# Macaron block on one core: the dense projection in fp16 parts set into the end of attention, and the QKV bias as rows of TensorE's accumulation

## What is computed

```
x = x + 0.5 * ffn(layernorm(x))
x = x + attn(layernorm(x))
x = x + 0.5 * ffn(layernorm(x))

ffn:  W = base + mean|w - base| * sign(w - base)          (for w1, w2, w3; inner width 1792)
      silu(h @ W1.T) * (h @ W3.T) @ W2.T
attn: qkv = h @ w_qkv.T + b_qkv                           (768 columns: 32 query heads, 8 key and 8 value heads of 16)
      q, k = rope(q), rope(k);  p = softmax(causal(q @ k.T / 16));  ctx = p @ v
      out = ctx @ w_dense.T + b_dense                     (512 x 512)
```

## Time and profile before

| | |
|---|---|
| median of 3 runs | 1591.55 us (1591.51 to 1592.71) |
| profiled execution, its own time | 1593.44 us |
| span of the profiled execution | 1591.7 us |
| PE / DVE / ACT / POOL busy | 1468.1 / 886.1 / 629.0 / 151.2 us |
| QKV stage (first QKV matmul to last evicted tile) | 531.48 to 618.42 |
| first score piece | 626.90 |
| VectorE ends groups 0, 1, 2 and 15 | 654.81, 682.22, 707.80, 1040.40 |
| iterations 16 and 17 begin; first projection matmul | 1041.27; 1075.04 |
| second feed-forward block begins | 1143.78 |

### The profile page before, as it was taken

The page is one execution under the profiler, slowest core; times in us unless marked ns, Lnnn a source line. Parts: engine busy times, 40 slices in busy tenths (PEclk is TensorE's granted clock), DMA queues, the critical chain, the costliest instruction groups (busy, mean ns, idle before and its releaser), DMA issues.

```text
span 1591.7 us, 24945 instructions
## 1 busy us (share of the span) xinstructions
PE 1468.1 (92%) x9552; PEld 660.3 (41%) x9552; DVE 886.1 (56%) x1387; ACT 629.0 (40%) x887; POOL 151.2 (10%) x217
## 2 busy tenths in 40 slices
PE   0778999899999895799999999989999999999998
PEld 0233444344445453334343434324444444444443
DVE  7979432432444587899999999923431422412212
ACT  4464111121222133388888888771211212112111
POOL 0320000000000243012121212210000000000000
PEclk9989999899999987599999999999999999999999
DMA  9501800000000000000000000024000000000000
GB/s 388 195 0 53 353 0 0 1 0 0 1 1 0 1 1 34 1 3 2 2 2 3 2 2 2 2 94 185 0 0 0 27 0 0 27 0 0 27 0 27
DMA packets 16459, 57.38 MB, mean 36 GB/s; under 512 B 4848, under 2 KB 4848, under 8 KB 15856
## 3 DMA queue, kind: packets, MB, share of 16 engines
q1 hardware_dynamic: 16368, 56.11, 9.1%
HBM read 40.63 MB, written 15.20 MB: 35 GB/s over the span
## 4 chain that ended last, share of the span: by engine, by line
PE 80%; DVE 12%; ACT 4%; issue 3%; DMA 1%; POOL 0%; DVEq 0%; SPq 0%; ACTq 0%; POOLq 0%
PE ps L1222 32%; PE ps L1243 16%; PE ps L1478 9%; PE ps L1393 7%; PE ps L1459 5%; PE ps L1576 3%; PE ps L1269 2%; PE ps L1216 1%; DVE w_all L870 1%; DVE rowmax L1110 1%; PE ps L1488 1%; PE ps L1355 1%; DVE w_raw L829 1%; DVE wbase L864 1%; ACT parts_q L665 1%
## 5 line engine op out<-in xcount | busy, mean ns | idle before, releaser
L1222 PE MATMUL ps<-xt_hi,w_all 128*128 128x512 f16 x896 | 284.3, 390 | 41.4 <-DVE w_all L870 19.3
L693 ACT ACTIVATE probs<-ps 128x1024 f32<-128x1024 f32 (+3 forms) x384 | 294.2, 814 | 48.7 <-PE ps L1459 45.7
L1110 DVE TENSOR_REDUCE rowmax<-ps 128x2 f32<-128x1024 f32 (+3 forms) x208 | 237.0, 1140 | 16.0 <-PE ps L1401 7.5
L958 DVE SCALAR_TENSOR_TENSOR hb<-ps,scal,silub 128x512 f32<-128x512 f32 x56 | 42.0, 750 | 266.6 <-PE ps L1222 266.6
L1393 PE MATMUL ps<-ka,qa 48*128 48x512 f16 (+3 forms) x768 | 165.6, 345 | 15.4 <-DVE rowmax L1110 9.2
L1222 PE MATMUL ps<-xt_lo,w_all 128*128 128x512 f16 x448 | 174.6, 390 | 0.0
L1478 PE MATMUL ps<-probs,vs 128*32 128x512 f32 (+3 forms) x1536 | 164.5, 500 | 1.6 <-ACT ctx_sb L712 1.1
L1222 PEld LDWEIGHTS ps<-xt_hi,w_all 128*128 128x128 f16 (+1 forms) x896 | 89.7, 100 | 155.5 <-issue 41.3
L1114 DVE TENSOR_REDUCE rowmax<-ps 128x1 f32<-128x512 f32 x192 | 131.1, 683 | 16.3 <-PE ps L1393 13.5
L1459 PE MATMUL ps<-qa,ka 50*128 50x512 f16 (+3 forms) x768 | 133.2, 330 | 3.7 <-ACT probs L693 2.8
L1243 PE MATMUL ps<-w32b_all,hhib 128*128 (+1 forms) x448 | 133.3, 379 | 0.0
(11 more groups left out here) (148 smaller groups left out, 2151.7 us busy)
## 6 DMA issues: line engine op xcount, KB each, us to landing
spill<-w_all SPq DMA_DIRECT2D x1, 10752.0 KB, 28.8
w32b_all<-spill SPq DMA_DIRECT2D x1, 7168.0 KB, 19.6
x<-x_in SPq DMA_DIRECT2D x4, 1024.0 KB, 5.4
y_out<-x SPq DMA_DIRECT2D x4, 1024.0 KB, 4.2
wbase<-m1t SPq DMA_DIRECT2D x4, 896.0 KB, 12.6
w_raw<-w1t SPq DMA_DIRECT2D x4, 896.0 KB, 14.1
wbase<-m3t SPq DMA_DIRECT2D x4, 896.0 KB, 24.3
w_raw<-w3t SPq DMA_DIRECT2D x4, 896.0 KB, 24.3
```

The lines of the kernel that those rows point to most:

```text
L693: nc.scalar.activation(probs[u % PBUF][:, 2 * pair:2 * pair + 2, 0:q1 - q0], wide(("scores", g, (u, pair)))[:, :, 0:q1 - q0], ACT.Exp, sca ...
L958: nc.vector.scalar_tensor_tensor(out=bufs["h"][u][:, :], in0=ps[:, UP, :], scalar=scal[:, 1:2], in1=bufs["silu"][u][:, :], op0=ALU.mult, o ...
L1110: nc.vector.tensor_reduce(dst, src, AX.X, ALU.max).then_inc(pair_taken, 1)
L1222: last = mm(ps[:, bank, :], w[a][:, k, bass.ts(t, P)], xt[b][:, k, :], start=(k == 0 and n == 0), stop=(k == HB - 1 and n == 2))
```

## The change

The change has two parts.

**The QKV bias.** VectorE's `add_bias` goes. Two fp16 rows' worth of bias (`brow`, 64 partitions: the high part and the remainder) are made by three VectorE instructions late in chunk 2, and `qkv(i)` begins each half with one more matmul of `row_ones` by `brow`. ScalarE's new `take_raw(i)` evicts the tile with the scale, ahead of `v_all(i)` in its order. In chunk 1 the maximum over the bias moves ahead of `power_of_two(3)`, and one small operation is added. `along(i)` waits for the low parts of tile i-2 too.

**The dense projection.** `wd` is held as two fp16 parts and the context too, in three passes: 12 matmuls of 512 columns for a tile. The maximum over `wd` is a VectorE instruction after iteration 0 (`dense_bound`), the scale a chain of nine after iteration 1 (`dense_scale`); GpSimd waits for the maximum ahead of its loop. GpSimd makes the high parts in iteration 2 (`dense_high`, two instructions for each of four blocks, between `copy_v(2)` and `mask_unit(1, 2)`) and the low parts in iteration 3 (`dense_low`, one for each of four, at the same place); SyncE moves them into place with four transfers after group 4's. The column of ones that gives the softmax sums is scaled by GpSimd. TensorE's and VectorE's iterations 16 and 17 are written out with tiles 0 to 7 of the projection between the pieces of attention, with one PSUM bank for the transposes and one for the results; VectorE makes both parts of these tiles' contexts. Tiles 8 to 15 follow attention, with ScalarE making the high part and VectorE the low one.

The diff, without semaphore declarations and with the written-out order cut:

```diff
-    mrow = at("mrow", [8 * SEQ_TILES, P], F16, C0 + 6144)
...
-    wd = at("wd", [P, HB, HID], F32, R0)
+    wd_raw = at("wd_raw", [P, HB, HID], F32, R0)
+    wd_at = [at(f"wd_at{i}", [P, 2, HID], F16, a) for i, a in enumerate((D0 + 6144, D0 + 14336, B0 + 30720, C0 + 6144))]
+    wd = [at(f"wd_{n}", [P, HB, HID], F16, R0 + 4096 * i) for i, n in enumerate(("hi", "lo"))]
...
-    ctx_t = [at(f"ctx_t{i}", [P, HB, P], F32, R0 + 10240 + i * 2048) for i in range(2)]
+    ctx_t = [[at(f"ctx_t{n}{i}", [P, HB, P], F16, R0 + 10240 + i * 2048 + j * 1024) for j, n in enumerate(("hi", "lo"))]
+             for i in range(2)]
...
+    def rows_bank(i):
+
+        return PAIR_BANK if i < SEQ_TILES else PAIR_BANK + i % 2
+
+    def dense_bank(i):
+
+        return PAIR_BANK + 1 if i < SEQ_TILES else i % 2
...
+            if g == 4:
+                sp.wait_ge(wdlo_ready, HB)
+                for i in range(2):
+                    for n in range(2):
+                        sp.dma_start(wd[i][:, 2 * n:2 * n + 2, :], wd_at[2 * i + n][:, :, :]).then_inc(wd_placed, 16)
 
...
+                chain(nc.gpsimd.memset(vs[i][:, :, HEAD:HEAD + 1], 1.0))
+                nc.gpsimd.tensor_scalar(vs[i][:, :, HEAD:HEAD + 1], vs[i][:, :, HEAD:HEAD + 1], wc[:, 4, 4:5], None,
+                                        ALU.mult).then_inc(ones_ready, 1)
...
+        def dense_high(n):
+
+            if n == 0:
+                pool.wait_ge(wd_scaled, 1)
+            chain(nc.gpsimd.tensor_scalar(wd_raw[:, n, :], wd_raw[:, n, :], wc[:, 3, 3:4], None, ALU.mult))
+            nc.gpsimd.tensor_copy(wd_at[n // 2][:, n % 2, :], wd_raw[:, n, :]).then_inc(wdhi_ready, 1)
+
+        def dense_low(n):
+
+            pool.wait_ge(wdhi_ready, n + 1)
+            nc.gpsimd.tensor_tensor(out=wd_at[2 + n // 2][:, n % 2, :], in0=wd_raw[:, n, :], in1=wd_at[n // 2][:, n % 2, :],
+                                    op=ALU.subtract).then_inc(wdlo_ready, 1)
+
+        pool.wait_ge(part_ready, 5)
+        nc.gpsimd.partition_all_reduce(allr[:, 3, 1:2], part[:, 3, 1:2], P, RMAX).then_inc(allr_ready, 1)
         for k in range(GROUPS + 2):
             mask_unit(k - 2, 7)
             mask_unit(k - 2, 8)
             mask_unit(k - 1, 0)
             mask_unit(k - 1, 1)
             copy_v(k)
+            if k == 2:
+                for n in range(HB):
+                    dense_high(n)
+            if k == 3:
+                for n in range(HB):
+                    dense_low(n)
...
+        def take_raw(i):
+            act.wait_ge(qkv_full, i + 1)
+            if i >= 2:
+                act.wait_ge(v_ready, i - 1)
+                act.wait_ge(rot_ready, i - 1)
+                act.wait_ge(turned_ready, 2 * (i - 1))
+            b0 = 2 * (i % 2)
+            nc.scalar.activation(qkv_raw[i % 2][:, :].rearrange("p (s n) -> p s n", s=2), ps[:, b0:b0 + 2, 0:QKV // 2],
+                                 ACT.Copy, scale=scal[:, 3:4]).then_inc(raw_ready, 1)
...
-        def take_ctx_t(i):
+        def context_high(i):
             act.wait_ge(dt_full, i + 1)
-            if i >= 2:
-                act.wait_ge(dense_full, i - 1)
-            nc.scalar.copy(ctx_t[i % 2][:, :, :].rearrange("p a b -> p (a b)"), ps[:, 4 + i % 2, :])\
-                .then_inc(ctx_t_ready, 1)
-
-        for i in range(TOKEN_TILES):
-            take_ctx_t(i)
+            act.wait_ge(dense_full, i - 1)
+            nc.scalar.copy(ctx_t[i % 2][0][:, :, :].rearrange("p a b -> p (a b)"), ps[:, rows_bank(i), :])\
+                .then_inc(ctx_hi_ready, 1)
+
+        for i in range(SEQ_TILES, TOKEN_TILES):
+            context_high(i)
...
+                    dve.wait_ge(tables_loaded, 48)
+                    chain(nc.vector.tensor_reduce(bqmax[:, :], bq[:, :], AX.X, ALU.max, apply_absolute_value=True))
+                    chain(nc.vector.tensor_scalar(wc[:, 3, 1:2], bqmax[:, :], 1.0 / 64, allr[:, 3, 1:2], ALU.mult, ALU.max))
                     power_of_two(3)
...
                     assert steps[0] == WQ_READY, steps[0]
-                    dve.wait_ge(tables_loaded, 48)
-                    chain(nc.vector.tensor_reduce(bqmax[:, :], bq[:, :], AX.X, ALU.max, apply_absolute_value=True))
+                    chain(nc.vector.tensor_scalar(scal[:, 5:6], wc[:, 3, 3:4], XS / M_UNIT, None, ALU.mult))
...
+                    nc.vector.memset(row_ones[:, :], M_UNIT / 32).then_inc(brow_ready, 1)
+                    dve.wait_ge(brow_ready, 2)
+                    nc.vector.scalar_tensor_tensor(out=brow[32:64, :], in0=bq[32:64, :], scalar=scal[32:64, 5:6],
+                                                   in1=brow[32:64, :], op0=ALU.mult, op1=ALU.subtract).then_inc(brow_ready, 1)
                 for t in (IT - 2, IT - 1):
...
-        def add_bias(i):
-            dve.wait_ge(qkv_full, i + 1)
-            if i >= 2:
-                dve.wait_ge(v_ready, i - 1)
-                dve.wait_ge(turned_ready, 2 * (i - 1))
-            b0 = 2 * (i % 2)
-            nc.vector.scalar_tensor_tensor(
-                out=qkv_raw[i % 2][:, :].rearrange("p (s n) -> p s n", s=2), in0=ps[:, b0:b0 + 2, 0:QKV // 2],
-                scalar=scal[:, 3:4], in1=bq[:, :].rearrange("p (s n) -> p s n", s=2), op0=ALU.mult,
-                op1=ALU.add).then_inc(raw_ready, 1)
-
         def along(i):
             dve.wait_ge(raw_ready, i + 1)
+            if i >= 2:
+                dve.wait_ge(qklo_ready, 2 * (i - 1))
             factor = cos[:, i % SEQ_TILES, :].unsqueeze(1).to_broadcast([P, ROT // HEAD, HEAD])
...
                 along(i)
...
-        for k in range(GROUPS + 2):
+        def dense_bound():
+
+            dve.wait_ge(wd_loaded, 32)
+            nc.vector.tensor_reduce(part[:, 3, 1:2], wd_raw[:, :, :].rearrange("p t n -> p (t n)"), AX.X, ALU.max,
+                                    apply_absolute_value=True)\
+                .then_inc(part_ready, 1)
+
+        def dense_scale():
+
+            dve.wait_ge(allr_ready, 9)
+            chain(nc.vector.tensor_copy(wc[:, 3, 1:2], allr[:, 3, 1:2]))
+            power_of_two(3)
+            chain(nc.vector.tensor_tensor(out=scal[:, 4:5], in0=wc[:, 3, 4:5], in1=wc[:, 4, 4:5], op=ALU.mult))
+            nc.vector.tensor_copy(wc[:, 3, 1:2], allr[:, 3, 1:2]).then_inc(wd_scaled, 1)
+
+        for k in range(GROUPS):
...
-
-
-        dve.wait_ge(wd_loaded, 32)
+            if k == 0:
+                dense_bound()
+            if k == 1:
+                dense_scale()
+
...
+        def context_high(i):
+            dve.wait_ge(dt_full, i + 1)
+            if i >= 2:
+                dve.wait_ge(dense_full, i - 1)
+            nc.vector.tensor_copy(ctx_t[i % 2][0][:, :, :].rearrange("p a b -> p (a b)"), ps[:, rows_bank(i), :])\
...
+        def context_low(i):
+            dve.wait_ge(ctx_hi_ready, i + 1)
+            hi, lo = (t[:, :, :].rearrange("p a b -> p (a b)") for t in ctx_t[i % 2])
+            nc.vector.tensor_tensor(out=lo, in0=ps[:, rows_bank(i), :], in1=hi, op=ALU.subtract).then_inc(ctx_lo_ready, 1)
+
+        def add_dense(i):
             dve.wait_ge(dense_full, i + 1)
             dve.wait_ge(bias_ready, i + 1)
-            nc.vector.tensor_tensor(out=x[:, i, :], in0=ps[:, i % 2, :], in1=x[:, i, :], op=ALU.add).then_inc(x2_ready, 1)
+            nc.vector.scalar_tensor_tensor(out=x[:, i, :], in0=ps[:, dense_bank(i), :], scalar=scal[:, 4:5], in1=x[:, i, :],
+                                           op0=ALU.mult, op1=ALU.add).then_inc(x2_ready, 1)
+
+        context_high(0)
...
+        bias_x(0)
+        bias_x(1)
+        context_high(1)
+        context_low(1)
+        bias_x(2)
+        bias_x(3)
+        add_dense(0)
+        context_high(2)
+        context_low(2)
+        bias_x(4)
+        bias_x(5)
...
+        normalise(15, 1)
+        add_dense(7)
+        context_low(SEQ_TILES)
+        for i in range(SEQ_TILES, TOKEN_TILES):
+            if i + 1 < TOKEN_TILES:
+                context_low(i + 1)
+            add_dense(i)
             if i == 8:
                 layer_norm(8)
             if i in (12, 13):
...
             if i == 1:
...
+                   start=True, stop=False)
                 for k in range(HB):
                     for n, (a, b) in enumerate(PASSES):
                         last = mm(ps[:, 2 * (i % 2) + s, 0:QKV // 2], xt[a][:, k, j * P:(j + 1) * P],
-                                  wq[b][:, k, s * QKV // 2:(s + 1) * QKV // 2],
-                                  start=(k == 0 and n == 0), stop=(k == HB - 1 and n == 2))
+                                  wq[b][:, k, s * QKV // 2:(s + 1) * QKV // 2], start=False,
+                                  stop=(k == HB - 1 and n == 2))
...
-        for k in range(GROUPS + 2):
+        for k in range(GROUPS):
...
             b, tt = divmod(i, SEQ_TILES)
-            if i >= 2:
-                pe.wait_ge(ctx_t_ready, i - 1)
+            if tt % 4 == 0:
+                pe.wait_ge(single_taken, taken(("ctx", GROUPS * (b + 1) // BATCH - 1, tt // 4)))
+            if i == 0:
```

(71 more changed lines are left out.)

131 lines of the change are left out of this document (119 added, 12 removed).

## The result

The changed kernel takes 1614.59 us (median; 1610.61 to 1619.24) against 1591.97 for the kernel before beside it: a ratio of 1.0142, 95% interval 1.0128 to 1.0156. The forecast was 1587.5, a little faster. Two executions of all that are reported here took far longer (2167.0 us of the kernel before, 2510.19 of experiment 5), and the ratios leave them out. Its lines L511, L518, L519 and L524 are GpSimd's mask, `dense_high`'s scaling and cast, and `dense_low`; L1505 is the bias matmul, L1509 the other QKV matmuls, L1607 `values`, L1588 `scores_t`, L1721 `project`, L719 ScalarE's `take_raw`.

A forecast was written before the change was run, and what follows sets the result against it. It took VectorE to bound the QKV stage, a TensorE-VectorE ring attention, and TensorE the feed-forward blocks. Gains of 8.3 and 9.4 us less preparation and stops summed to -4.0 us from 1591.55: 1587.5 us, range 1577 to 1598.

The forecast's parts named there:

- the nearer row: GpSimd, iteration 2: each `dense_high` instruction priced as the mask, 0.634 us, not at `copy_v`'s 1.16, the dearest bound.
- the stop of 2.8: Attention, iteration 2: `dense_high` delays the mask, so TensorE stops 2.8 us ahead of `values(1, 2)`; 2.8 to 6.9 with iteration-2 bounds.
- The first rival: GpSimd's instructions cost as `copy_v`'s elements, TensorE slow after both stops: gain eaten, +9.0 us, 1596.5; chance 0.17.
- First feed-forward block +2.2: Bias preparation in chunks 1 and 2: exposed VectorE operations add 2.2 us (1.5 to 4).
- QKV stage -8.3: QKV stage: TensorE becomes the bound, 26 matmuls of 0.163 us a tile, 4.23; gain 8.3 us (0 to 12).
- `dense_bound` +1.9: VectorE after attention's iteration 0: the maximum over `wd` adds 1.9 us (1 to 2.3).
- `dense_scale` +1.4: VectorE in attention's loop: nine chained operations, 1.7 us, taken as adding 1.4 us (0 to 1.7).
- Start of attention, 0: From the last evicted QKV tile into the first iterations: no change counted, up to 5.5 us to win if the clock holds.
- Iteration 3, +2.9: Attention, iteration 3: `dense_low` on GpSimd, 5.1 us, makes the mask 2.9 us late (2.5 to 4.5).
- Slow returns, one of 2.5: TensorE after the two GpSimd stops and chunk 2's short one: one return at low clock, +2.5 us (0 to 7).
- Tail, 54.3: Iterations 16 and 17 with projected tiles 0 to 7: 54.3 us (52 to 58) instead of 33.8, +20.5.
- Tiles 8 to 15, 38.8: Dense stage behind attention: 38.8 us (35 to 41) instead of 68.7, -29.9; with the tail, -9.4.

The follow-up runs named there:

- experiment 5: The QKV bias part of the change alone, with its 64-row bias matmuls, in the kernel before: 1591.08 us, ratio 0.9990.
- experiment 1: The changed kernel with one tiny GpSimd addition (128x1) right behind the all-reduce of the dense weight's bound: 1608.63 us, ratio 1.0099.
- experiment 3: The changed kernel with the bias in 128 partitions instead of 64, so its matmul has 128 rows: 1610.97 us, ratio 1.0111.
- experiment 2: experiment 1 with GpSimd's dense-weight preparation moved ahead of mask_unit(k-1, 0), into its idle time in iterations 2 to 4: 1596.07 us, ratio 1.0010.
- 7: experiment 2 with the statistics of the second feed-forward block's first LayerNorm taken in the tail: 1584.53 us, ratio 0.9961.
- experiment 6: experiment 2 with the tail's projection quarters issued in pairs, 16 groups of six matmuls instead of 32 of three: 1586.20 us, ratio 0.9968.

## Why the prediction was wrong

The step that failed is GpSimd in iteration 2: "I take the nearer row, the mask: 8 x 0.634 = 5.1 us", and the stop of 2.8 from it. Two things were wrong in it. Four of the eight instructions are scalings, of 1.57 us, dearer than even the far row's 1.16; the four casts, 0.61, are at the near row. Together they take 8.9 us (712.27 to 721.16), and that this lies within the bound of 8 x 1.16 = 9.3 is luck. And 7.37 us for the first arithmetic after an all-reduce stood in no term, nor in the bounds; experiment 1 shows it. Together they made 14.0 us of 2.8. The first rival had the place and the sign; it said that over 0.9 us for an instruction decides, and it was priced without the wait. A page of the Trainium skill that I had not used for this names a cost of this kind: "GPSIMD Engine Reference", section "Instruction dispatch", has the first call of freshly loaded code pay about 6 us that no instruction of the profile shows. Here it was 6.7 to 7.7; that code is loaded in it, no row shows.

The other terms, forecast and measured in the profiled pair:
- First feed-forward block +2.2: right for the stops, 6.54 and 2.29 us for 6.29 and 0.34. The QKV stage starts only 0.6 us later, because 0.9 was gained at the very start, ahead of the change's first instruction, and the lower clock behind the first stop ended sooner and took 0.8 less (granted clock 0.94 for 0.71 between 290 and 295 us).
- QKV stage -8.3: -2.4. ScalarE and the slow return were right, and nearly so the stop ahead of `qkv(6)` (5.1 forecast, 4.28). "26 x 0.163" took a 64-row matmul at its neighbours' rate; it costs 0.2 us more, 6 us in the stage. With 128 rows the term is right to 0.3 us (experiment 3).
- `dense_bound` +1.9: +2.6; `dense_scale` +1.4: 1.6, and 4.4 more in this execution (3.0 in experiment 2, none in 7) for a slow clock that I had tied only to longer stops.
- Start of attention, 0: right, 36.3 us from the last evicted tile to the end of iteration 0 for 36.4. Only iteration 0 was at 0.50 throughout in the kernel before; iteration 1 has 0.70 in the earlier trace rows, not 0.50.
- Iteration 3, +2.9: +5.2. `dense_low` took 4.50 us instead of 5.1, the stop was 2.21 and the lower clock behind it the rest.
- Slow returns, one of 2.5: they came after both GpSimd stops (3.9 and 2.9), behind `dense_scale` (4.4), and in the tail (1.5). The stop behind which the 4.4 came was of 1.58 us only.
- Tail, 54.3: 61.5. Stops were 4.7 for 5.5. 32 groups at 0.12 make 3.8 (0.10 to 0.13 by experiment 6), the clock 1.5; the remaining 2.7 us I can't place.
- Tiles 8 to 15, 38.8: 37.8, with a stop of 5.97 for 6.2 and the slow return.

So both named gains were real but small: 2.4 us of 8.3 in the QKV stage, where the shape of one matmul took the rest, and 3.2 of 9.4 in tail and dense stage. The loss came from 12 small instructions in another engine's queue, the wait ahead of the first of them and the lower clock behind.
